# Dispatch of an audio tower: norm powers by root and Newton step, gates first, norm on ScalarE, stream added on TensorE

## The reference

```python
h = tok(x)                                        # patch embedding, norm
h = h + attn(layernorm(h))                        # state space layer with a memory
h = h + ffn(layernorm(h))                         # mixture of experts, one expert a token
h = h + attn2(layernorm(h)); h = h + ffn2(layernorm(h))

# end of attn: memory read and gate
k = y_ssm @ key_W + key_b
h_mem = (k @ M) @ recall_W + recall_b
gate = sigmoid(y_ssm @ gate_W + gate_b)
y = y_ssm + gate * h_mem

# start of ffn: the expert of each token and its place among that expert's tokens
raw = einsum('bnd,de->bne', x, w_gating)
probs = softmax(raw); idx1 = argmax(probs)
pos1 = (cumsum(one_hot(idx1)) - one_hot(idx1)) * one_hot(idx1)
xn = layernorm(expert_in, gamma)                  # a second norm, on top of layernorm(h)
```

## Time and profile before

| | |
|---|---|
| time, median of 3 runs | 821.22 us (820.77 to 825.59) |
| time of the profiled execution | 817.75 us |
| its span, first to last instruction | 815.9 us |
| mean granted clock of TensorE | 0.874 |
| busy over the span: PE, PEld | 620.8 us (76%), 472.5 us (58%) |
| busy over the span: DVE, ACT, POOL | 621.7 us (76%), 517.0 us (63%), 278.7 us (34%) |

### The profile page before, as it was taken

One profiled execution on the slowest core, in us unless ns is written; L12 is line 12 of the kernel. 1 busy time (PEld: TensorE's weight loads), 2 busy tenths in 40 slices (PEclk: granted clock), 3 DMA queues, 4 the chain that ended last, 5 costly groups with the idle time before them and its releaser, 6 DMA issues.

```text
span 815.9 us, 10867 instructions
## 1 busy us (share of the span) xinstructions
PE 620.8 (76%) x3090; PEld 472.5 (58%) x3091; DVE 621.7 (76%) x1275; ACT 517.0 (63%) x821; POOL 278.7 (34%) x321
## 2 busy tenths in 40 slices
PE   6996751735628173569768899987899999999997
PEld 3564651735628173565546699844556656666565
DVE  1788598999999999999886122267798898896853
ACT  1488899989998999993233134442565565565442
POOL 0464200000000100000387244416357657664642
PEclk9996886958777695869686799999999999999999
DMA  5371042355444455540611366320000000000000
GB/s 183 113 282 63 1 87 51 67 100 106 74 87 87 88 101 102 92 74 6 223 32 37 105 177 187 93 67 1 1 1 9 2 10 10 0 10 10 2 10 18
DMA packets 26384, 56.50 MB, mean 69 GB/s; under 512 B 4204, under 2 KB 15573, under 8 KB 25861
## 3 DMA queue, kind: packets, MB, share of 16 engines
q0 software_dynamic: 5728, 24.56, 16.0%
q1 hardware_dynamic: 19848, 30.80, 12.2%
q10 hardware_dynamic: 764, 0.62, 0.2%
HBM read 29.91 MB, written 10.17 MB: 49 GB/s over the span
## 4 chain that ended last, share of the span: by engine, by line
PE 48%; ACT 18%; DVE 15%; issue 11%; POOL 3%; DMA 2%; POOLq 1%; SPq 1%; ACTq 1%; DVEq 0%
PE psum L2113 6%; PE psum L1895 4%; PE psum L1897 4%; PE psum L1896 4%; PE psum L1809 4%; ACT s_R L899 3%; PE psum L2028 3%; ACT s_R L889 3%; PE psum L2100 3%; PE psum L2036 3%; ACT s_R L894 3%; PE psum L2203 2%; PE psum L2102 2%; PE psum L2101 2%; POOL x_sorted L698 2%
## 5 line engine op out<-in xcount | busy, mean ns | idle before, releaser
L1895 PE MATMUL psum<-s_xn_lo,s_split_hi 128*128 128x368 f32 x256 | 94.9, 371 | 132.5 <-ACT s_R L924 132.5
L1895 PEld LDWEIGHTS psum<-s_xn_lo,s_split_hi 128*128 128x128 f32 x256 | 55.1, 215 | 135.8 <-ACT s_R L924 135.2
L683 POOL DMA_DIRECT2D s_xnfm<-s_R x14 | 17.1, 1219 | 249.9 <-DVE s_R L1310 249.9
L1305 DVE TENSOR_TENSOR_SCAN s_R<-s_R 128x2944 f32<-128x2944 f32 x15 | 94.4, 6292 | 0.7
L1896 PE MATMUL psum<-s_xn_hi,s_split_lo 128*128 128x368 f32 x256 | 92.2, 360 | 0.0
L1897 PE MATMUL psum<-s_xn_hi,s_split_hi 128*128 128x368 f32 x256 | 91.9, 359 | 0.0
L1069 ACT ACTIVATE s_R<-psum,s_cols 128x368 f32<-128x368 f32 x96 | 50.1, 565 | 65.9 <-PE psum L2102 65.8
L2113 PE MATMUL psum<-s_R 128*128 128x368 f32 x256 | 90.5, 484 | 0.0
L742 POOL TENSOR_TENSOR s_R<-s_R 128x368 f32<-128x368 f32 x47 | 54.0, 1148 | 39.5 <-DVE s_R L1601 19.3
L931 ACT ACTIVATE s_R<-psum,s_cols 128x736 f32<-128x736 f32 x64 | 56.0, 875 | 14.2 <-PE psum L1897 10.7
L779 POOL TENSOR_TENSOR s_R<-s_R 128x368 f32<-128x368 f32 x48 | 46.5, 969 | 53.9 <-DVE s_R L1737 53.0
(11 more groups left out here) (263 smaller groups left out, 1608.9 us busy)
## 6 DMA issues: line engine op xcount, KB each, us to landing
s_xnfm<-s_R POOLq DMA_DIRECT2D x14, 1472.0 KB, 10.5
s_R<-in_w SPq DMA_DIRECT2D x28, 256.0 KB
s_R<-in_xg SPq DMA_DIRECT2D x7, 744.0 KB, 4.1
x_sorted<-in_x_init SPq DMA_DIRECT2D x1, 5082.0 KB
s_wBC<-in_wBC SPq DMA_DIRECT2D x8, 256.0 KB, 2.8
s_R<-in_v SPq DMA_DIRECT2D x2, 1024.0 KB
s_R<-x_sorted SPq DMA_DIRECT2D x28, 66.0 KB
s_R<-in_w SPq DMA_DIRECT2D x1, 1536.0 KB, 6.6
```

The lines of the kernel that those rows point to most:

```text
L1305: dve.tensor_tensor_scan(bufB[:, u], ra[:, u], bufB[:, u], 0.0, ALU.mult, ALU.add).then_inc(ra_free, 1)
L1895: pe.matmul(bank(c), w_hi[:, s, u, k, :], xn_lo[:, a:b], start=True, stop=False)
```

## The change

- GpSimd computes the powers of chunks 0 and 1 only. For the other six VectorE makes the same two values for a pair together (`moments`), ScalarE takes their square root (`roots`, 92 x 16 elements), and VectorE makes the reciprocal and one Newton step (`power`), and -mean x factor (`shiftC`). GpSimd's scatters of a pair are now eight in a row.
- ScalarE applies the norm (`normed_c`: Identity with scale and bias, four operations), in VectorE's place.
- The products for the gates (`gate_product`) of all chunks are made before the loop, and their sigmoids too, except that of chunk 7, which follows the first norm. The gates lie in xfm, which is free by then. The counts move to bank 3.
- For chunks 2 to 7 TensorE adds the stream: `stream_in(c)` multiplies H by the identity (512 columns) into the bank, and `memory_onto(c)` adds cF by four products with the identity, in place of transposes. ScalarE copies the sum back to H (`keep_stream`). Chunks 0 and 1 are summed on VectorE as before (`first_sum`).
- ScalarE loads the table of the square root once, in the first pair.
- The keep-busy products of the pairs are gone; five stand in the last pair ahead of its counts, where before they stood in the third pair behind its counts.

```diff
             pool.wait_ge(fill_done, 2 * 16)
             rstd_c(0)
             rstd_c(1)
-            rstd_c(2)
             for i in range(NP):
                 pool.wait_ge(nC.xs1_ready, 2 + 2 * i + 2)
                 pool.wait_ge(slot_ready, i + 1)
-                if i < NP - 1:
-                    scatter(i, 0, 1)
-                    rstd_c(2 * i + 3)
-                    scatter(i, 1, BP)
-                    if i < NP - 2:
-                        rstd_c(2 * i + 4)
-                else:
-                    scatter(i, 0, BP)
+                scatter(i, 0, BP)
...
+            def normed_c(c):
+                u = c % 2
+                act.wait_ge(shift_ready, SHIFT0 + (c + 1 if c < 2 else 2 + c // 2))
+                act.wait_ge(nC.xT_ready, c + 1)
+                for j in range(CB):
+                    ins = act.activation(xs[:, u, j, :], H[:, c * CB + j, :], ACT.Identity,
+                                         scale=rstd[:, u, j:j + 1], bias=shiftC[:, u, j:j + 1])
+                ins.then_inc(nC.xs_ready, 1)
...
+            def keep_stream(c):
...
+                act.wait_ge(cT_ready, c + 3)
+                act.activation(seqs(H, c).rearrange("p j d -> p (j d)"), psum[0:L, 4 + c % 2, 0:CB * D], ACT.Copy)\
+                    .then_inc(cT_free, 1)
+
+            def roots(i):
...
+                act.wait_ge(nC.var_ready, 2 + i)
+                act.activation(root[:, :, :, :].rearrange("p u k j -> p (u k j)"),
+                               pa2[:, :, :, :].rearrange("p u k j -> p (u k j)"), ACT.Sqrt)\
+                    .then_inc(nC.rstd_ready, 1)
...
             for i in range(NP):
-                for c in (2 * i + 2, 2 * i + 3):
-                    if c < NCH:
-                        gate_of(c)
-                for c in (2 * i, 2 * i + 1):
-                    logits_in(c)
-                for c in (2 * i, 2 * i + 1):
-                    stream_row(c)
+                normed_c(2 * i)
+                if i == 0:
+                    gate_of(NCH - 1)
+                    logits_in(0)
+                    normed_c(1)
+                else:
+                    normed_c(2 * i + 1)
+                    logits_in(2 * i)
+                keep_stream(2 * i + 2)
+                logits_in(2 * i + 1)
+                keep_stream(2 * i + 3)
+                if i == 0:
+                    load_table(ACT.Sqrt, 0)
+                stream_row(2 * i)
+                roots(i + 1)
+                stream_row(2 * i + 1)
...
+            def power(i):
...
+                v, r, f, out = (x[:, :, :, :].rearrange("p u k j -> p (u k j)") for x in (pa2, recip, fix, rs2))
+                dve.wait_ge(nC.rstd_ready, 2 + i)
+                dve.wait_ge(nC.var_ready, 2 + i)
+                step.add(dve.reciprocal(r, root[:, :, :, :].rearrange("p u k j -> p (u k j)")))
+                step.wait()
+                step.add(dve.scalar_tensor_tensor(f, v, -0.5, r, ALU.mult, ALU.mult))
+                step.wait()
+                step.add(dve.tensor_tensor(f, f, r, ALU.mult))
+                step.wait()
+                dve.wait_ge(nC.xs1_ready, 2 + 2 * i)
+                step.add(dve.scalar_tensor_tensor(out, f, 1.5, r, ALU.add, ALU.mult))
+                step.wait()
+                dve.scalar_tensor_tensor(shiftC[:, :, :], mv[:, :, :, 0], -1.0, rstd[:, :, :], ALU.mult, ALU.mult)\
+                    .then_inc(shift_ready, 1)
...
             for i in range(NP):
-                normed(2 * i)
+                if i == 0:
+                    first_shift(0)
                 memory_read(2 * i + 2)
-                normed(2 * i + 1)
+                if i == 0:
+                    first_shift(1)
                 memory_read(2 * i + 3)
-                onto_stream(2 * i + 2)
+                moments(2 * i + 2)
+                moments(2 * i + 3)
                 if i == 0:
                     dve.wait_ge(rt_const, 9 * 16)
                 choose(i)
-                stream_sum(2 * i + 3)
+                power(i + 1)
                 place(i)
-                if 2 * i + 3 < NCH:
-                    norm_stats(dve, nC, step, seqs(H, 2 * i + 3), 1, True)
...
             for i in range(NP):
                 norm_transposes(pe, nC, 0, 2 * i, (6, 7))
-                memory_tm(2 * i + 2)
+                memory_onto(2 * i + 2)
+                norm_transposes(pe, nC, 1, 2 * i + 1, (6, 7))
+                if i == 0:
+                    stream_in(3)
+                memory_onto(2 * i + 3)
                 logits(2 * i)
-                norm_transposes(pe, nC, 1, 2 * i + 1, (6, 7))
                 logits(2 * i + 1)
-                memory_tm(2 * i + 3)
+                read_memory(2 * i + 4)
+                read_memory(2 * i + 5)
+                stream_in(2 * i + 4)
+                stream_in(2 * i + 5)
                 if i == 0:
                     pe.wait_ge(rt_const, 9 * 16)
                     pe.wait_ge(ones_ready, 1)
-                if i < NP - 1:
-                    keep_busy_3(1)
+                    pe.wait_ge(sig_ready, NCH)
+                if i == NP - 1:
+                    keep_busy_3(5)
                 counts(i)
-                if i == NP - 2:
-                    keep_busy_3(5)
-                read_memory(2 * i + 4)
-                read_memory(2 * i + 5)
```

More of the change, by code:

```diff
@@ L345, in audio_tower @@
         Y = xnfm
-        sig = take(2, CT)
+        sig = xfm
         cF = take(2, CT)
@@ L394, in audio_tower @@
         cnt_mm, cum_ready, cnt_read = sem("cnt_mm"), sem("cum_ready"), sem("cnt_read")
+        CNT = 3
+        inv8 = take(2, CB, parts=L)
+        root = take(2, 2, CB, parts=L)
+        recip = take(2, 2, CB, parts=L)
+        fix = take(2, 2, CB, parts=L)
+        shiftC = take(2, CB, parts=L)
+        shift_ready, SHIFT0 = x_split, 2 * NCH + 1
+        gate_mm, GATE0 = yT_ready, 2 + NCH
         tile_ready, slot_ready, id_ready = sem("tile_ready"), sem("slot_ready"), sem("id_ready")
@@ L980, in _ @@
             sum_out(3)
+            for c in range(2, NCH - 1):
+                gate_of(c)
             for i in range(NP):
-                for c in (2 * i + 2, 2 * i + 3):
-                    if c < NCH:
-                        gate_of(c)
-                for c in (2 * i, 2 * i + 1):
-                    logits_in(c)
-                for c in (2 * i, 2 * i + 1):
-                    stream_row(c)
+                normed_c(2 * i)
[14 more added lines that the diff above has]
+                stream_row(2 * i + 1)
             act.wait_ge(rt_a, 1)
@@ L1394, in memory_read, with first_sum @@
                 dve.tensor_tensor(cF[:, u], cF[:, u], fm(Y, c), ALU.add).then_inc(cF_ready, 1)
[L1396 to L1398 removed]
+            def first_sum(c):
                 dve.wait_ge(cT_ready, c + 3)
@@ L1410, in normed @@
-            def normed(c):
-                dve.wait_ge(nC.rstd_ready, c + 1)
-                norm_apply(dve, nC, c % 2, c, True)
+                u = c % 2
+                dve.wait_ge(cT_free, c + 3)
+                for j in range(CB):
+                    step.add(dve.bn_stats(stat[:, u, j, :], seqs(H, c)[:, j, :]))
+                step.wait()
+                for j in range(CB):
+                    ins = dve.bn_aggr(mv[:, u, j, :], stat[:, u, j, :])
+                step.add(ins)
+                if u:
+                    step.wait()
+                    var = mv[:, :, :, 1]
+                    step.add(dve.tensor_scalar(pa2[:, :, 0, :], var, EPS, None, ALU.add))
+                    step.add(dve.tensor_scalar(pa2[:, :, 1, :], var, 1.0 + EPS, EPS * EPS, ALU.mult, ALU.add))
+                    step.wait()
+                    step.add(dve.reciprocal(inv8[:, :, :], pa2[:, :, 0, :]))
+                    step.wait()
+                    dve.tensor_tensor(pa2[:, :, 1, :], pa2[:, :, 1, :], inv8[:, :, :], ALU.mult)\
+                        .then_inc(nC.var_ready, 1)
@@ L1942, in memory_tm, with stream_in, memory_onto @@
                     ins = pe.transpose(bank_tm(4 + c % 2)[:, j, :], cF[:, c % 2, j * L:(j + 1) * L], ident[:, :])
+                ins.then_inc(cT_ready, 1)
+            def stream_in(c):
+                if not c < NCH:
+                    return
+                pe.wait_ge(cT_free, c + 1)
+                pe.matmul(psum[0:L, 4 + c % 2, 0:CB * D], ident[0:L, 0:L], seqs(H, c).rearrange("p j d -> p (j d)"),
+                          start=True, stop=False)
+            def memory_onto(c):
+                if not c < NCH:
+                    return
+                pe.wait_ge(cF_ready, c + 1)
+                for j in range(CB):
+                    ins = pe.matmul(bank_tm(4 + c % 2)[:, j, :], cF[:, c % 2, j * L:(j + 1) * L], ident[:, :],
+                                    start=False, stop=(j == CB - 1))
                 ins.then_inc(cT_ready, 1)
@@ L1974, in _ @@
             memory_tm(1)
-            read_memory(2)
-            read_memory(3)
+            for c in (2, 3):
+                read_memory(c)
+                gate_product(c)
```

(3 more changed lines are left out.)

60 lines of the change are left out of this document (37 added, 23 removed).

## The result

The changed kernel takes **827.42 us** (median of 20 runs, 823.51 to 829.51), the kernel before 821.0 us (20 runs, 819.38 to 825.59) in the same sessions. The ratio is **1.0061, 95% interval 1.0046 to 1.0077**: 5.0 us slower with 1.3 us to either side (the two medians are 6.4 us apart), under the one per cent that was set as the bound of "same". The forecast was 827.1 us. The profiled run has a span of 826.2 us and a time of 828.04.

The account below looks back on a forecast made before the run. It took GpSimd as ending the stage before; after, a loop through VectorE, ScalarE and TensorE at a mixed clock. Period 13.1 and last part 13.2 put the last scatter at 458.0, plus 5.9 on 821.22: 827.1 us, range 818 to 833.

Parts of the forecast that it names:

- 5.9 us forecast: Dispatch stage: the last scatter was to start at 458.0 in place of 452.14, plus 5.9 us.
- The signs: Dispatch stage: scatters in eights with waits, VectorE waiting for the stream copy, clock near 0.66, last counts behind five products.
- The milestones: Dispatch stage times: first slots 410.0, third 436.2, last power's end 435.3, last slots 448.5, last scatter 458.0.
- The 5.24 and 0.97 us: Last scatter's start to the next stage's first product, 5.24; first slots to first scatter, 0.97; both kept unchanged.
- What is removed: 8.6 us.: GpSimd loses six of eight powers; the five between scatters cost 8.6 us of its queue.
- My own sum: Dispatch stage: first slots, periods, last part and last scatters worked out to 458.0, against 452.14 before.
- The period at 2.4 GHz, 10.7 us: Loop of a pair through VectorE and ScalarE: 4.4, moments 3.25, choose 1.85, power 1.1; above GpSimd's 9.8.
- The period at 1.2 GHz, 14.3 us: Loop of a pair with TensorE at half clock: its work of 16.1 us, less some 1.8 for overlaps, sets the period.
- The mix: Rounds of the dispatch stage at the earlier clock, 68% at 1.2 GHz: a period of 10.7 + 0.68 x 3.6 = 13.1 us.
- The last part, 13.2 us: Last power to last slots, five keep-busy products ahead of the counts: 10.3 us at full clock, 14.5 at half, 13.2 mixed.
- Rival A: TensorE keeps 2.4 GHz in the dispatch stage: last scatter at 448.3, minus 3.8, 817.4 us; chance 0.18.
- The table load: ScalarE's square-root table load in the first pair: 1.28 us that cost nothing; by the skill page's 2.66, 0.9 more.

Follow-up runs that it names:

- run 1: Changed kernel with the last round's five filler products issued behind its counts instead of ahead: 823.87 us, 1.0030.
- Run 5: Kernel before with GpSimd's six powers of chunks 2 to 7 left out, waits and signals kept: 821.86 us, 0.9995.
- run 11: Changed kernel with GpSimd making the powers of chunks 2 to 7 again, no roots or Newton steps: 831.11 us, 1.0126.
- Run 12: Changed kernel with three filler products more behind the counts of each of the first three rounds: 817.43 us, 0.9958.
- run 6: Changed kernel with 20 filler products in place of 15 behind the stage's last counts: 824.33 us, 1.0036.
- run 2: Changed kernel with each round's counts issued ahead of the next round's two stream products: 825.69 us, 1.0041.
- Run 4: Changed kernel with the stream's sum of chunks 2 to 7 back on VectorE, using transposes again: 821.37 us, 0.9992.
- run 10: run 9's kernel with two filler products more behind the counts of each of the first three rounds: 815.43 us, 0.9934.
- run 9: run 8's kernel with three more filler products at the stage's end, 18 in place of 15: 816.64 us, 0.9939.
- run 7: Kernel before with 18 filler products in place of 15 behind the stage's last counts: 820.8 us, 0.9988.
- run 3: Changed kernel with the edits of run 1 and run 2 together: 819.83 us, 0.9975.
- run 8: Changed kernel with the stream's sum back on VectorE and the last round's five fillers behind its counts: 816.2 us, 0.9929.

## Why the prediction was right, and where it was not

**The time** came out 0.3 us from the forecast, and the mechanism is the one it gave: GpSimd loses 8.6 us of powers, waits for slots in place of them, and the slots come at the pace of a loop through TensorE at a mixed clock. That it came so close is in part luck (by the ratio the changed kernel would stand at 826.2 on the 821.22 of the forecast, still close). Of the 5.9 us forecast 5.25 stood ahead of the first slots, and of the 6.86 measured in the trace 4.9 do, but profiles with the same instructions put these slots anywhere from 408.1 to 411.4. Behind them a wait of 3.2 us that had no price and a period at 2.4 GHz that was priced too long went against each other. The signs are all there: scatters in eights with waits ahead of them, VectorE waiting for the stream copy (4.7 us), a mean clock of 0.68, the last counts behind the fillers, the next stage's first product at 464.2 (said: near 463).

**The milestones.** First slots 409.7 (said 410.0 for a stretch at 1.2 GHz; it was at that clock only from 399.2 to 402.6, and run 1, at 2.4 GHz up to its first slots, has 408.55 where 407.6 was said, since its second norm ends at 399.7 and not 398.5), third 436.6 (436.2), last power ends 435.7 (435.3), last slots 449.6 (448.5), last scatter 459.0 (458.0). The 5.24 and 0.97 us held: 5.23 and 0.97.

**"What is removed: 8.6 us."** GpSimd's account was right, its place in the chain was not. I took GpSimd as what ended the stage and VectorE as nearly full. Run 5 shows that in the kernel before the powers alone were worth 1 to 2.5 us in the traces and nothing that the medians tell: VectorE's 12.7 us a round stood right behind. My own sum escaped this only because it worked out the new slots from the start and did not subtract 8.6 from the old time. Once VectorE was relieved, the same powers were worth 5 us (run 11).

**The period at 2.4 GHz, 10.7 us.** Run 12 measured 10.1 in the round that was at this clock throughout. The terms: norms 3.18 (3.3), power 1.05 (1.1), stream copy 0.59 (0.60); the rest, some 0.4, is not accounted for; overlaps that I had not taken off are a guess. So it is nearer GpSimd's 9.8 than I had it.

**The period at 1.2 GHz, 14.3 us.** The changed kernel's round at this clock took 15.2 (15.8 in run 1; in run 6 the same round, partly at 2.4 GHz, 13.9). The prices were good, as these groups of it show (start us, us, engine, line), the first two at 1.2 GHz:
```profile
411.01 1.99 PE L2031 MATMUL psum<-s_ident,s_R 128*92 128x128 f32 x8
415.12 2.52 PE L2039 MATMUL psum<-s_smallw,s_R 128*92 128x6 f32 x16
...
430.01 1.40 PE L2039 MATMUL psum<-s_smallw,s_R 128*92 128x6 f32 x16
```
The sum onto the stream was priced 2.05, two stream products cost 3.39 (two at 1.83). What was short is the queue: I wrote that the stream products stand ahead of the counts and gave that no price of its own. It is 3.2 us in the second round, and run 2 gives 2.8 of it back. Run 4 shows the other side: with the sum on VectorE a round at 1.2 GHz takes 11.2.

**The mix.** A mean of the two periods, 13.1, was right as a mean (15.2 and 11.7; the last round, with its fillers, 13.0) and hid how far rounds lie apart: with the same instructions the third slots came 9.9 us behind the second in run 6, where the clock was 2.4 GHz for 7 us of them. The clock alone does not make a round slow, either: at 1.2 GHz throughout it took 12.4 us in run 2 and 11.2 in run 4.

**The last part, 13.2 us from the last power to the last slots**, took 13.9. The five fillers, priced at 3.3 us at 2.4 GHz, took 5.79, of which 3.6 lay behind the choice.

**Rival A** would have held at a full clock. Its numbers, third slots 429.0 and last scatter 448.3, are near what run 12 shows, 428.3 and 447.9, at 817.4 us, with a mean clock of 0.91. It was wrong for this kernel for about the reason given, that TensorE would not be at work all the time; where, ahead of the transposes and of the counts, the prediction did not say. The rule of the Trainium skill, TensorE: Matmul & The Clock Gate, "Part 4: PE-mode transpose", that stood with it is not decided. What the prediction drew from it did not come: with products in place of transposes the mean clock was 0.68 beside 0.66. Run 4, back to transposes and at 0.50 from 397.6 to 438.5, fits the rule, but it also has less to do in all, and run 10, with the same transposes and two fillers a round, was at 2.4 GHz from 409.3 to 416.1. Run 12 changed only the idle time.

**The table load** was hidden, as said. It took 1.28 us, and ScalarE's next operation began 0.02 us behind it. The Trainium skill, ScalarE: Activation LUTs, "What ACT_TABLE_LOAD costs", has the same 1.28 for the load and 1.38 more for a drain, 2.66 in all; this trace shows nothing of the drain. The row scalings behind it end at 407.7, the power's write that needs them starts at 408.24 without a wait:
```profile
403.78 1.28 ACT L818 ACT_TABLE_LOAD   x1
...
405.08 0.20 ACT L818 ACTIVATE s_unused<-s_ident 128x1 f32<-128x1 f32 x1
...
406.46 1.26 ACT L252 ACTIVATE s_R<-s_xs,s_rs 92x128 f32<-92x128 f32 x4
...
408.24 0.17 DVE L1479 SCALAR_TENSOR_TENSOR s_rs<-s_R 92x16 f32<-92x16 f32 x1
```

**What stays open.** No run undoes the norm's move to ScalarE or the early gates, so how the 4.9 us ahead of the first slots divide between the parts of the change is read from one trace and not shown. The fillers of each round, the last fillers behind the counts, and a filler count at the end that fits the earlier slots were not run together; run 12 still idles 4.93 us ahead of the next stage and starts it at 1.2 GHz.

## What to carry to other kernels

Taking work from the engine that ends a stage gives only the distance to the next full engine: look whether that one ever waits before counting the gain (here VectorE waited for a power once, 1.38 us, and the 8.6 us were worth 2.3 at most by the medians). When work is moved to an in-order queue, price what stands behind it there, at the slower clock: two groups ahead of tiny counts cost about as much as the change lost. Look at the start of a stage by itself: most of this loss lay ahead of the first slots, where the new path is longer and nothing runs beside it yet. And where TensorE idles a few microseconds in every round, try products without a purpose in that gap. It paid in the changed kernel (run 12) and showed nothing in run 10; in the kernel before it was not tried.

## What the runs showed of the hardware

- TensorE's granted clock changed the length of a round as much as moves of work did: 10.1 us at 2.4 GHz (run 12), 15.2 at 1.2 GHz in the changed kernel, with the same instructions but for three fillers, and 11.2 at 1.2 GHz with the stream's sum on VectorE (run 4). It fell in idle times of 2.7 us (run 12) and of 2.4 and 2.8 (changed kernel, at 409.4 and 433.4), at the end of one of 1.6 (at 399.2) and just behind one of 1.95 (at 426.5); it held over 0.5 us in run 12. Once, at 450.4 in the changed kernel, it fell with no idle time above 0.4 us since it had risen at 447.0, so idle time is not all that it hangs on.
- The same at the stage's border: after 1.03 us or less of idle time the next stage began at 2.4 GHz, after 1.96 us or more it ran at 1.2 GHz for 10 to 12 us and took some 3 to 4 us longer in the trace. The medians showed nothing certain of it, in the changed kernel, in the kernel before or in run 9.
- A scatter by slots costs GpSimd 1.22 us of its queue in every run (the first of a round up to 1.6). From the start of the last one to the next stage it took 5.2 us in both kernels and in runs 2, 4, 5, 7, 11 and 12, and 5.7, 5.5 and 6.8 us in runs 1, 3 and 8. Why is not known: in the last three the last eight scatters followed those before them without a pause, but in the kernel before and in run 7 they did so too.
